# A chain of seven attention layers on one core: v by one matmul, k and v spread through DRAM, the attention output turned a phase earlier

## The reference, cut to what matters

```
L0_SELF   x += attn(ln(x), causal)             L0_CROSS  x += attn(ln(x), ctx);  x += mlp(ln(x))
L1_CROSS  x += attn(rms(x), ctx) with rope on q and k
L2_SELF   x  = ln(x + attn(x, causal, pad))    L2_CROSS  x = ln(x + attn(x, ctx, pad)); x = ln(x + mlp(x))
L3_SELF   x += attn(ln(x))                     L3_CROSS  x += attn(ln(x), ctx);  x += mlp(ln(x))
attn = softmax(q k^T / sqrt(8)) v per head, then an output projection;  mlp: 128 -> 512, gelu, -> 128
```

## Time and profile before

| | us |
|---|---|
| median of 3 runs (lowest, highest) | 2583.32 (2580.74, 2585.79) |
| the profiled execution, its own time | 2582.77 |
| its span, first to last instruction | 2580.9 |
| mean granted clock of TensorE | 0.989 |
| busy: TensorE matmuls / weight loads | 2395.7 / 1834.9 |
| busy: VectorE / ScalarE / GpSimd | 1869.4 / 1910.6 / 1390.4 |

### The profile page before, as it was taken

The page is one execution under the profiler, slowest core; times in us unless marked ns, Lnnn a source line. Parts: engine busy times, 40 slices in busy tenths (PEclk is TensorE's granted clock), DMA queues, the critical chain, the costliest instruction groups (busy, mean ns, idle before and its releaser), DMA issues.

```text
span 2580.9 us, 112383 instructions
## 1 busy us (share of the span) xinstructions
PE 2395.7 (93%) x42093; PEld 1834.9 (71%) x42093; DVE 1869.4 (72%) x4641; ACT 1910.6 (74%) x4734; POOL 1390.4 (54%) x3556
## 2 busy tenths in 40 slices
PE   3799999999999899999999989999999989999986
PEld 2477767777777677777777766777777767777765
DVE  3477787777767778777776778777777777877753
ACT  1486758888887666888887765788888766688865
POOL 3254336775554444876554434687555434487632
PEclk9799999999999999999999999999999999999989
DMA  5000000000000010000000000000000000000000
GB/s 108 11 21 24 24 23 16 15 15 20 21 21 25 23 27 18 15 15 17 22 21 22 26 23 22 17 16 15 19 21 21 15 13 15 17 15 15 17 16 14
DMA packets 123713, 54.13 MB, mean 21 GB/s; under 512 B 35680, under 2 KB 122465, under 8 KB 123169
## 3 DMA queue, kind: packets, MB, share of 16 engines
q1 hardware_dynamic: 118176, 43.81, 6.8%
q10 hardware_dynamic: 4128, 1.65, 0.3%
q0 software_dynamic: 864, 1.28, 0.3%
HBM read 13.06 MB, written 4.19 MB: 7 GB/s over the span
## 4 chain that ended last, share of the span: by engine, by line
PE 42%; POOL 23%; issue 22%; ACT 8%; DVE 2%; POOLq 1%; SPq 1%; DMA 0%; DVEq 0%; ACTq 0%
PE ps_scores_t L781 8%; PE ps_scores L761 4%; PE ps_turn L911 4%; PE ps_wide L899 4%; PE ps_out L793 4%; POOL x_bias L604 3%; PE ps_wide L853 3%; PE ps_turn L814 2%; PE ps_wide L836 2%; PE ps_out L802 2%; POOL pre_rstd L547 2%; PE ps_turn L822 2%; POOL post_rstd L547 2%; PE ps_wide L837 2%; ACT probs L694 2%
## 5 line engine op out<-in xcount | busy, mean ns | idle before, releaser
L1103 DVE TENSOR_REDUCE row_max<-ps_scores 128x16 f32<-128x1024 f32 x448 | 548.2, 1224 | 359.0 <-PE ps_scores L769 188.6
L694 ACT ACTIVATE probs<-ps_scores_t 128x512 f32<-128x512 f32 x896 | 535.2, 597 | 84.0 <-PE ps_scores_t L781 72.9
L1113 DVE TENSOR_TENSOR shifted<-ps_scores,row_max 128x512 f32<-128x512 f32 x896 | 576.6, 685 | 15.4
L781 PE MATMUL ps_scores_t<-ident,shifted 128*128 128x128 f32 x3584 | 569.9, 282 | 17.3 <-ACT probs L694 11.3
L781 PEld LDWEIGHTS ps_scores_t<-ident,shifted 128*128 128x128 f32 x3584 | 394.9, 142 | 64.0 <-issue 11.4
L761 PE MATMUL ps_scores<-k_slots,qk_rows 32*64 32x256 f32 x7168 | 312.6, 405 | 15.1 <-issue 12.9
L793 PE MATMUL ps_out<-probs,v_ones 128*32 128x64 f32 x14336 | 289.6, 221 | 12.9 <-ACT probs L694 12.9
L685 ACT COPY attn_t<-ps_turn 128x128 f32<-128x128 f32 x448 | 118.7, 265 | 207.9 <-PE ps_turn L814 206.8
L544 POOL TENSOR_TENSOR mlp_var_eps<-mlp_mean_var,eps 128x1 f32<-128x1 f32 x128 | 24.5, 192 | 448.9 <-DVE mlp_mean_var L1054 448.9
L793 PEld LDWEIGHTS ps_out<-probs,v_ones 128*32 128x32 f32 x14336 | 232.8, 110 | 38.0 <-issue 16.4
L680 ACT COPY pv_sb<-ps_out 128x256 f32<-128x256 f32 x448 | 166.9, 373 | 123.2 <-PE ps_out L793 119.6
(11 more groups left out here) (173 smaller groups left out, 4662.3 us busy)
## 6 DMA issues: line engine op xcount, KB each, us to landing
k_slots<-qk_rows SPq DMA_DIRECT2D x1792, 16.0 KB, 1.8
x_in<-in_x SPq DMA_DIRECT2D x64, 64.0 KB, 1.9
ctx_in<-in_ctx SPq DMA_DIRECT2D x64, 64.0 KB, 2.0
out<-x SPq DMA_DIRECT2D x64, 64.0 KB, 1.6
w<-in_L_xattn_W SPq DMA_DIRECT2D x2, 256.0 KB, 6.7
raw<-in_L_xattn_w_fc SPq DMA_DIRECT2D x1, 256.0 KB, 3.4
raw<-in_L_xattn_w_fc ACTq DMA_DIRECT2D x1, 256.0 KB, 5.4
w<-in_L_xattn_W ACTq DMA_DIRECT2D x1, 256.0 KB, 7.0
```

Source lines behind the costliest of these rows:

```text
L694: nc.scalar.activation(probs[:, u, :, :], ps_scores_t[:, :] .rearrange("p (h t) -> p h t", h=4), ACT.Exp, scale=SCALE).then_inc(probs_read ...
L781: ins = nc.tensor.transpose(ps_scores_t[:, h * P:(h + 1) * P], shifted[:, j % 2, u, h * P:(h + 1) * P], ident[:, :])
L1103: v.tensor_reduce(row_max[:, :].rearrange("p (g n) -> p g n", n=SLOTS), ps_scores[:, :, 0:256].rearrange("p g (n k) -> p g n k", k=LEN), A ...
L1113: v.tensor_tensor(shifted[:, j % 2, u, :].rearrange("p (g n k) -> p g n k", n=SLOTS, k=LEN), ps_scores[:, 2 * u:2 * u + 2, 0:256].rearrang ...
```

## The change

v becomes one matmul like q and k; q, k, v lie side by side in `ps_wide` and are copied to `qkv_rows` by one ScalarE instruction. The biases of q and k move from that copy to a bf16 matmul ahead of q and k. SP writes k and v rows to a DRAM buffer whose rows are zero around them (zeroed once, 2 MB), waits for the landing, and reads k back through a window that shifts each row into its slot (256 KB) and v in two DMAs into `v_ones`, whose last dimension is now the head pair. Context, x, attention output and MLP input are all turned at the end of a phase into one bank and copied by one instruction to `turned`. The steps of a unit move: values and the attention turn in j+2 (`VALUES`), project in j+3 (`OUT`), MLP in j+4, j+5, j+6. VectorE normalises before the residuals. The lines of the mask are the same in both kernels.

```diff
-TURN_OUT = 2
-MLP_TURN, UP, DOWN = 3, 4, 5
+VALUES, OUT = 2, 3
+MLP_TURN, UP, DOWN = 4, 5, 6
...
-        v_ones = sb("v_ones", [P, RING, 2, HEADS // 2, 32])
+        v_ones = sb("v_ones", [P, RING, 2, 32, HEADS // 2])
+        kv_dram = nc.dram_tensor("kv_dram", (RING, (P + 1) * KV_ROW), F32).ap()
...
-                    for slot in range(SLOTS):
-                        sp.dma_start(k_slots[slot:P:SLOTS, j % RING, slot, :],
-                                     qk_rows[slot:P:SLOTS, j % RING, 1, :]).then_inc(k_landed[j % RING].sem, 16)
+                        sp.wait_ge(rows_ready.sem, rows_ready.at(r, j))
+                        sp.dma_start(rows[:, KV_HOME::SLOTS, :], qkv_rows[:, c, 1:3, :]).then_inc(kv_written[c].sem, 16)
+                    sp.wait_ge(kv_written[c].sem, kv_written[c].at(r, j))
+                    sp.dma_start(k_slots[:, c, :, :], k_windows(c)).then_inc(k_landed[c].sem, 16)
+                    v_home = rows[:, KV_HOME + SLOTS, :].rearrange("(b k) x -> k b x", b=2)
+                    for e in range(2):
+                        sp.dma_start(v_ones[64 * e:64 * e + 64, c, :, HD * e:HD * e + HD, :],
+                                     v_home[:, :, 64 * e:64 * e + 64]).then_inc(v_landed[c].sem, 16)
...
+                sp.wait_ge(zeroed, 1)
+                for c in range(RING):
+                    sp.dma_start(kv_rows(c).rearrange("p n x -> p (n x)"), zeros[:, :]).then_inc(rows_cleared, 16)
...
+                def copy_turned(r, j):
+                    act.wait_ge(turns_ready.sem, turns_ready.at(r, j))
+                    if exists(r, j + TURN_IN) and layer_of(j + TURN_IN) == L0_SELF:
+                        nc.scalar.copy(ctx_t[:, stream_of(j + TURN_IN), :], ps_turn[:, 0:P]).then_inc(ctx_turned, 1)
+                    parts = turned_parts(r, j)
+                    lo, hi = parts[0], parts[-1] + 1
+                    nc.scalar.copy(turned[:, lo:hi, :], ps_turn[:, lo * P:hi * P]
+                                   .rearrange("p (n t) -> p n t", t=P)).then_inc(turned_copied.sem, 1)
...
                 def phase(r, j):   # ScalarE after: copy_pv(j-2), exps(j-1,0), copy_rows(j+2) or copy_rope_v,
                                    # exps(j-1,1), gelus(j-5), copy_turned(j)
...
-                                                       v_ones[:, j % RING, b, 4 * u + h, :],
+                                                       v_ones[:, c, b, :, 4 * u + h],
...
+                def qkv(r, j):
...
+                    if biased:
+                        nc.tensor.matmul(ps_wide[:, 0:2 * P], bias_parts[:, :],
+                                         bias_sel_bf[:, QK_BIAS[layer]:QK_BIAS[layer] + 2].unsqueeze(2)
+                                         .to_broadcast([P, 2, P]), start=True, stop=False)
+                    nc.tensor.matmul(ps_wide[:, Q_COLS], w_q[:, layer, :], tokens, start=not biased, stop=not biased)
+                    nc.tensor.matmul(ps_wide[:, K_COLS], w_k[:, layer, :], kv_tokens, start=not biased, stop=True)
...
+                    dst = ps_turn[:, 0:P] if layer == L1_CROSS else ps_wide[:, V_COLS]
+                    nc.tensor.matmul(dst, kv_tokens, w_v[:, layer, :], start=True, stop=True).then_inc(qkv_ready.sem, 1)
...
+                def turns(r, j):
+                    pe.wait_ge(residual_done.sem, residual_done.at(r, j - OUT))
+                    pe.wait_ge(mlp_residual_done.sem, mlp_residual_done.at(r, j - DOWN))
...
+                    if exists(r, j - VALUES):
+                        pe.wait_ge(attn_ready.sem, attn_ready.at(r, j - VALUES))
+                        ins = nc.tensor.transpose(ps_turn[:, 256:384], attn[:, :], ident[:, :])
+                    ins.then_inc(turns_ready.sem, 1)
...
+                    if exists(r, j):
+                        scores(r, j)
+                    if exists(r, j - VALUES):
+                        values(r, j - VALUES)
+                    if exists(r, j - 1):
+                        transposes(r, j - 1, 0)
+                    turned_free(r, j)
+                    if exists(r, j + QKV):
+                        qkv(r, j + QKV)
+                    if exists(r, j - VALUES):
+                        pv_t(r, j - VALUES)
+                    turn_bank_free(r, j)
+                    if has_mlp(r, j - DOWN):
+                        mlp_down(r, j - DOWN)
+                    if exists(r, j - OUT):
+                        project(r, j - OUT)
+                    if exists(r, j - 1):
+                        transposes(r, j - 1, 1)
+                    if has_mlp(r, j - UP):
+                        mlp_up(r, j - UP)
+                    if turned_parts(r, j):
+                        turns(r, j)
```

More of the change, by code:

```diff
@@ L69 @@
 GELU = {L0_CROSS: ACT.Gelu, L2_CROSS: ACT.Gelu, L3_CROSS: ACT.Gelu_apprx_tanh}
-Q_BIAS = {L0_SELF, L0_CROSS, L3_SELF, L3_CROSS}
-K_BIAS = {L0_SELF, L3_SELF, L3_CROSS}
 MASK = {L0_SELF: 0, L2_SELF: 1, L2_CROSS: 2}
+QK_BIAS = {L0_SELF: 12, L0_CROSS: 14, L3_SELF: 16, L3_CROSS: 18}
+N_BIAS = 20
+KV_ROW, KV_HOME = 2 * SLOTS * P, SLOTS - 1
+Q_COLS, K_COLS, V_COLS = slice(0, P), slice(P, 2 * P), slice(2 * P, 3 * P)
+CTX_TURN, H_TURN, ATTN_TURN, MLP_TURNED = range(4)
 def stream_of(j):
@@ L105, in has_mlp, with turns_of @@
     return exists(r, j) and layer_of(j) in MLP
+def turns_of(n):
+    return [part for part, there in ((H_TURN, in_program(n + TURN_IN)), (ATTN_TURN, in_program(n - VALUES)),
+                                     (MLP_TURNED, in_program(n - MLP_TURN) and layer_of(n - MLP_TURN) in MLP))
+            if there]
 class Norm:
@@ L146, in at, with __init__, total @@
         return r * self.round + (self.total(j) + short)
+class PhaseSignal:
+    def __init__(self, sem, happens):
+        self.sem, self.happens = sem, happens
+        self.table = {}
+    def total(self, n):
+        if n not in self.table:
+            self.table[n] = sum(self.happens(i) for i in range(-STATS, n + 1))
+        return self.table[n]
+    def at(self, r, j):
+        if isinstance(r, int):
+            return self.total(PER_ROUND * r + j)
+        return r * PER_ROUND + self.total(j)
 def build(nc, a, out):
@@ L249, in build, with turns_there @@
         setup_dve = sem("setup_dve")
-        first = {L0_SELF: 1}
+        ctx_turned = sem("ctx_turned")
+        def turns_there(n):
+            return 1 if turns_of(n) else 0
         with_mlp = {n: 1 for n in MLP}
@@ L614, in phase @@
                 def phase(r, j):
[L615 removed]
+                    out, down = j - OUT, j - DOWN
                     if exists(r, j + 1):
@@ L650, in copy_rows @@
-                def copy_rows(r, j, which, bias, done):
-                    layer = layer_of(j)
-                    src, dst = ps_wide[:, which * P:(which + 1) * P], qk_rows[:, j % RING, which, :]
-                    act.wait_ge(qkv_ready.sem, qkv_ready.at(r, j))
-                    if bias is not None:
-                        ins = nc.scalar.activation(dst, src, ACT.Identity, bias=bias[:, layer:layer + 1])
-                    else:
-                        ins = nc.scalar.copy(dst, src)
-                    ins.then_inc(done.sem, 1)
@@ new lines, in turn_bank_free, with mlp_down @@
+                def turn_bank_free(r, j):
+                    if exists(r, j + QKV) and layer_of(j + QKV) == L1_CROSS:
+                        pe.wait_ge(rope_v_ready.sem, rope_v_ready.at(r, j + QKV))
+                    if not turned_parts(r, j - 1):
+                        pe.wait_ge(residual_done.sem, residual_done.at(r, j - 1 - OUT))
+                        pe.wait_ge(mlp_residual_done.sem, mlp_residual_done.at(r, j - 1 - DOWN))
+                def mlp_down(r, j):
+                    pe.wait_ge(gelu_ready.sem, gelu_ready.at(r, j))
+                    for c in range(HCH):
+                        ins = nc.tensor.matmul(ps_turn[:, 256:384], gelu[:, c, :], w_2[:, MLP[layer_of(j)], c, :],
+                                               start=c == 0, stop=c == HCH - 1)
+                    ins.then_inc(mlp_y_ready.sem, 1)
@@ L799, in pv_t, with project @@
+                def project(r, j):
+                    nc.tensor.matmul(ps_turn[:, P:2 * P], turned[:, ATTN_TURN, :], w_o[:, layer_of(j), :],
+                                     start=True, stop=True).then_inc(y_ready.sem, 1)
                 def pv_t(r, j):
@@ L1000, in _ @@
                     step(v.tensor_copy(b_v_wide[:, i, :], b_v[:, layer:layer + 1].to_broadcast([P, P])))
-                for i in range(3):
-                    step(v.tensor_copy(b_1_wide[:, 32 * i:32 * i + len(MLP) * HCH], b_1[:, :]))
                 assert done[0] == SETUP_WIDE
```

417 lines of the change are left out of this document (170 added, 247 removed).

## The result

| | before | after |
|---|---|---|
| median of 4 runs, us (lowest, highest) | 2584.56 (2580.74, 2587.74) | **2703.1** (2697.68, 2714.57) |
| ratio, 95% interval | | **1.047** (1.0434 to 1.0507) |
| span of the profiled execution, us | 2580.9 | 2695.6 |
| mean granted clock of TensorE | 0.989 | 0.968 |

The account below looks back on a forecast made before the run. TensorE's own order was taken as the bound, VectorE close behind. Pairs -39, head and tail -16, setup and end +7 sum to -48; 6 given back, so 2582.8 us becomes 2540, range 2485 to 2680.

Parts of the forecast that it names:

- rows are ready 3.2 to 4.3 us into phase j ... 6 us of cover, so I count nothing: k and v through DRAM: rows wanted two phases on, about 10.5 us, so the 4.6 us trip was counted as nothing.
- The way of k: k's DRAM write and read on SP: 2.1 + 2.4 + 0.1 = 4.6 us.
- the 10.35 that I gave: Forecast time of two phases in the L2_SELF with L1_CROSS stage, in us.
- scores waiting for k: Sign that the forecast is wrong: scores wait for k's landing, the cover is gone; each us beyond 6 costs one per pair.
- rival 1: Strided v_ones slows the weight loads of values: 0.3 us a phase, +135 us, 2675 us, chance 0.22.
- the head: Head and tail pairs, 8.83 us before, become bound by k's way, 3.2 + 4.6 = 7.8: -16 us in 16 pairs.
- stage sums: Pair times per stage from TensorE's and VectorE's orders, 10.35 to 11.1 us, with +0.6 in L2_CROSS for its norm.
- Biases: bf16 bias matmul ahead of q and k in four of seven layers: 0.25 us each, ends 0 and 0.32.
- that rope phases with an MLP lose over a us: Pairs of L1_CROSS with L0_CROSS lose more than a us, as v no longer waits behind ScalarE's table load.
- the schedule of three stages without rope: Pair times: L3_SELF with L2_CROSS 11.0 us, L3_CROSS with L3_SELF 10.35, L0_SELF with L3_CROSS 10.8.
- my 10.80: Mean pair time forecast, 10.74 plus 0.06 for stage changes, against 10.98: 0.18 us in some 216 pairs, -39 us.
- Rival 2: ScalarE's one turned copy, behind gelu, delays the next q, k, v: 0.5 us x 190, 2635 us, chance 0.13.

Follow-up runs that it names:

- e3: Changed kernel with rope_sum moved right behind the second shift on VectorE, ahead of normalise and both residuals: 2615.62 us, ratio 1.0112.
- e9: Kernel before with only v_ones and v's weight columns in the changed kernel's strided order: 2605.91 us, ratio 1.0064.
- e5: Changed kernel with GpSimd's end of the pre-norm moved ahead of the end of the attention's post-norm: 2668.0 us, ratio 1.0336.
- e7: Changed kernel with rope_sum behind the second shift, statistics behind both residuals, pre-norm's end ahead of the attention's post-norm: 2567.14 us, ratio 0.9958.
- e2: Changed kernel with every unit's k sent by four copies inside SBUF, only v through DRAM: 3029.84 us, ratio 1.1717.
- e10: Changed kernel with k's read from DRAM issued ahead of v's write, in rope units alone: 2751.57 us, ratio 1.0621.

## Why the prediction was wrong

1. **The step that failed is "rows are ready 3.2 to 4.3 us into phase j ... 6 us of cover, so I count nothing".** That holds for units whose rows ScalarE copies. A rope unit's rows are ready when `rope_sum` ends, 3.40 + 3.45 = 6.85 us after the scores in the changed kernel, because the change puts normalise, the residual and (which I overlooked) the post-norm's statistics ahead of it; before it was 5.09. The way of k took 5.93 us, not 4.6: a second wait of SyncE for v's write, and a landing of 3.0 to 3.3 for 256 KB against my 2.4. With both, 12.8 stands against the 10.35 that I gave (with my 4.6 it would still be 11.45), and by my own rule each us beyond the cover is one a pair. The DMA rows, against the earlier trace rows:

```profile
k_slots<-kv_dram SPq DMA_DIRECT2D x448, 256.0 KB, 3.0
kv_dram<-qkv_rows SPq DMA_DIRECT2D x384, 128.0 KB, 2.1
v_ones<-kv_dram SPq DMA_DIRECT2D x896, 32.0 KB, 2.6
kv_dram<-qkv_rows SPq DMA_DIRECT2D x128, 64.0 KB, 1.7
```

The prediction named the sign to look for, scores waiting for k; it gave that case no chance. It costs 92 us by e3's ratio, more than half of the 163 us between forecast and result. That 2703 us lies near rival 1's 2675 is chance: e9 gives the strided loads 17 us.

The same way mis-sized the head. There I had the right bound, the way of k, with 3.2 + 4.6 = 7.8 us a pair. In the changed kernel's trace the scores start within 0.05 us of k's landing in each of the first seven pairs, 5.2 to 5.3 us behind its write (64.44 to 69.71), and the next write starts some 4 us behind the scores (74.14): 9.3 us a pair. The head took 64.9 us for its first 14 phases, 63.5 before, and the tail alone gave 7, where I had -16 for the two.

2. **GpSimd was left out of the stage sums.** I gave each down phase of L2_CROSS +0.6 for VectorE's statistics ahead of the residual (0.5 measured: 1120.06 to 1120.53 in the changed kernel's trace) and did not ask who starts behind them. e5: 35 us.

3. **Biases**: 0.10 to 0.11 us instead of 0.25, which is the matmul without the step. The step of 0.30 in the earlier trace rows was not the change of type (what it was stays open); in the changed kernel bf16 loads follow at the usual distance (starts of four transposes, bias, q):

```profile
815.21 0.66 PE L821 MATMUL ps_scores_t<-ident,shifted 128*128 128x128 f32 x4
815.70 0.27 PE L846 MATMUL ps_wide<-bias_sel_bf,bias_parts 128*128 128x256 bf16 x1
815.81 0.39 PE L849 MATMUL ps_wide<-turned,w_q 128*128 128x128 f32 x2
```

4. **Strided loads, rival 1**: the way of it was right and its price was not, 0.3 us a phase by the rival and 0.04 to 0.07 measured (e9: 17 us in 448 phases). The forecast had this at nothing. Values and then transposes in the changed kernel, 0.67 us apart, against 0.61 in the earlier trace rows:

```profile
1028.78 0.61 PEld L809 LDWEIGHTS ps_out<-probs,v_ones 128*32 128x32 f32 x32 [0.20 <-issue]
1029.45 0.42 PEld L821 LDWEIGHTS ps_scores_t<-ident,shifted 128*128 128x128 f32 x4
```

5. **Right**: the price of the copies (384 columns 0.477 us, 0.49 forecast); that rope phases with an MLP lose over a us, once k is out of the way (12.33 to 10.76 in e7); the schedule of three stages without rope, 10.97 against 11.0 and 10.15 and 10.64 a little below their forecasts; L2_CROSS/L2_SELF missed, 11.65 against 11.1, by GpSimd's order and the statistics (10.65 in e7). L0_CROSS/L0_SELF has 10.79 in the last round (10.8 forecast, 11.04 before). Its mean of 11.56 holds a stall of some 5 us at the loop's seam, in two of the four rounds, that the kernel before has too: 5.5 us there. The 10.98 that I started from holds one such stall, 5.5 / 56 = 0.10 us a pair, and my 10.80 none, so over half of the 0.18 us a pair was never to be had. Rival 2 is out: TensorE's matmuls wait for the turned copy for under 4 us in the whole run.

One sum of the prediction is short of a term: the parts named for the phase of the earlier trace rows give 3.46 us, and 4.29 only with the 0.83 from the second transposes to the last turn. Four transposes and the two matmuls of `pv_t` fill 0.66 of it, so 0.17 is a hole.

What e7 leaves, 0.4% for the better, is smaller than the 1.7% forecast: L2_SELF/L1_CROSS still takes 10.63 against 9.68, bound now by the residual ahead of the turns (TensorE waits for it twice a pair, 1.7 us together, and never for k), as the prediction had it; and the change into L3_SELF/L2_CROSS takes 11.72 against 10.63, with 1.3 us a pair of waits for GpSimd's post-norm.

## What to carry to other kernels

When an edit lengthens a way that "has cover", the cover is to be counted for the unit that comes latest on that way, from the instruction that really produces its data, through every instruction and every wait of the queues it passes; a mean over the units hides it. An in-order queue that waits (SyncE here) joins units that have nothing to do with each other, so shortening one way can lengthen the next one's. When two engines' orders have been rewritten, the cheap trial is to move single lines: one move was worth 92 us here, and three brought the changed kernel from 4.7% behind the old one to 0.4% ahead.

## What was not expected of the hardware

- Issuing is not free: SyncE took 0.34 to 0.61 us for each DMA. Some took longer: in the changed kernel 16% of v's reads took over 1.3 times their median of 0.61, 1.23 us on average and 2.4 at most. Seven issues and one wait a phase made it the bound (e2, 1.17).
- v's write of 64 KB behind a 256 KB read in the same queue is confirmed later, 2.8 us against 2.2 behind a 64 KB write (e10, medians).
- A wait of 2 us on TensorE was followed by a granted clock of one half over the q, k, v matmuls, and over the rope units it was 0.5 us longer from scores to the first product (3.40 against 2.88 in e3): the wait fed itself.
- Weight loads of 32 columns 8 numbers apart took 151 ns on average, against 110 side by side, and only 0.065 us of that in 32 came through.
